# A memset between the scattered and gathered transfers, in place of waits, in an audio tower with a mixture of experts

## The chip, the cores and the metric

The kernel runs on one core of a Trainium2 chip. The metric is the device time of one execution in microseconds. It has five engines with a queue each: PE (matmul), DVE (vector), ACT (scalar), POOL (GpSimd) and SP, which here only issues DMAs. Transfers with a list of rows (indirect DMAs) are issued by POOL, the others by SP and ACT.

## The reference, cut to what matters

Tokens are 128 sequences of 63 positions with 64 channels. A depthwise convolution with a norm and an activation comes first, then a state-space block, then a mixture of 64 experts, of which each token uses two.

```python
def _L0_ffn_ref(x, Wr, br, W1, b1, W2, b2):
    logits = xf @ Wr + br
    topk_logits, topk_idx = jax.lax.top_k(logits, TOP_K)          # TOP_K = 2
    gates = jax.nn.softmax(topk_logits, axis=1)
    combine = jnp.zeros((T, E), xf.dtype).at[jnp.arange(T)[:, None], topk_idx].add(gates)
    for e in range(E):                                            # E = 64
        h = jax.nn.relu(xf @ W1[e] + b1[e])
        y = h @ W2[e] + b2[e]
        out = out + combine[:, e:e + 1] * y
...
h = _L0_tok_ref(x, ...)
h = h + _L0_attn_ref(_layernorm(h, axis=-1), ...)
h = h + _L0_ffn_ref(_layernorm(h, axis=-1), ...)
```

## The kernel before

Partitions are sequences, the free axis is positions and channels. The convolution and the state-space block (POOL, DVE, ACT and PE together) take the first half of the time. The change is in what follows.

**Routing.** The 63 positions are cut into eight groups of 8 (the last has 7) and into three shares, SHARES = (0, 16), (16, 40), (40, 63): groups 0 and 1, groups 2 to 4, groups 5 to 7. For each group ACT normalises, PE makes the logits, DVE picks the two best experts (`choose`, which counts s_hot up) and PE counts tokens for each expert. For each share DVE then computes where each token's row goes in a list sorted by expert (`slots_of`, `rows_of`: L1547 writes slot_i and counts s_slot up) and which expert each tile of that list belongs to.

**Scatter.** `send` (L625) has POOL write the rows of a share into its `sorted_rows` in DRAM: one indirect DMA for each position and choice, 128 rows of 256 bytes each, so 2 x 63 = 126 in all (32, 48 and 46 for the three shares). A share's rows may be read once its s_disp is full.

**Expert steps.** 80 steps, 24, 28 and 28 for the shares; a step takes two pairs of tiles of 128 rows. PE transposes the rows (`rows_T`, L887), multiplies with W1 (`hidden`, L897) two loops later and with W2 (`outputs`, L906) four loops later, so there are 84 loops. ACT copies (L1162) and applies half of the relu (L1167), DVE does the other half (L1595) and copies the outputs (`y_copy`, L1604), which counts s_dstep up. ACT issues the loads of sorted rows, a unit of two steps at a time and some steps ahead (`next_rows`): the first unit of the second share in loop 17, that of the third in loop 45, and there it waits for that share's s_disp. It also issues the store of each step's outputs to `expert_out`. SP loads the weights of each tile, 96.5 KB, 11 steps ahead at most.

**Gather.** For each share, POOL waits until all of its steps are stored (s_st), and then gathers the rows of `expert_out` back with one indirect DMA for each position and choice (L651), 126 again. Behind the steps PE and ACT make the bias part (s_cb), DVE adds it (L1653, s_cbc) and then adds the gathered rows times their gates (L1645, L1647), group by group of OUTS; SP stores.

**The pace.** POOL's order is scatter of shares 0, 1, 2, then gather of shares 0, 1, 2. Transfers are numbered d = 0 to 251 in this order. `keep_pace(d)` (L616) stands ahead of each: at six of the scatters it waits until a group has been chosen (GROUP_AT: transfer 18 for the third group, ..., 44 for the eighth), from d = 62 on at every second one it waits until the steps have come to (d - 60) x 80 / 153 (STEP_AT), and from 212 on at every third for a bias add (BIAS_AT). `Chain.link` (L137) makes an instruction count a semaphore up and makes the engine wait for the new count ahead of its next instruction.

Of the kernel before, what the change touches and what calls it, by code (L numbers as in the profile page):

```python
# [15 lines left out]
P = 128  # L16
# [3 lines left out]
L = 63  # L20
# [23 lines left out]
SHARES = ((0, 16), (16, 40), (40, L))  # L44
# [23 lines left out]
PAIR0, UNIT0, STEP0 = ([sum(v[:h]) for h in range(len(SHARES) + 1)] for v in (PAIRS, UNITS, STEPS))  # L68
# [4 lines left out]
IDS = 32  # L73


FIRST_STEP = 44
LAG = 16
EVERY = 2
GROUP_AT = {18: 3, 21: 4, 25: 5, 38: 6, 41: 7, 44: 8}
STEP_AT = {d: (d - FIRST_STEP - LAG) * STEP0[-1] // 153 for d in range(FIRST_STEP + LAG + EVERY, FIRST_STEP + LAG + 154, EVERY)}  # L80
BIAS_AT = {212 + 3 * q: q + 1 for q in range(CQ)}


# [39 lines left out]
def dve_rounds(steps):  # L123
    return steps + LATE - LAG_H
# [18 lines left out]
def build(nc, x, w, b, gamma, beta, alpha, A_log, D_param, scale, W_dt, b_dt, W_B, b_B, W_C, b_C,  # L143
# [5 lines left out]
    with ExitStack() as ctx:  # L149
        def sb(name, shape, dt=F32):  # L150
            return ctx.enter_context(nc.sbuf_tensor(name, shape, dt))

        def sem(name):
            return ctx.enter_context(nc.semaphore(name))
# [47 lines left out]
        tile_e = sb("tile_e", [P, len(SHARES)])  # L202
        te = sb("te", [1, len(SHARES) * P], I32)
        b2w = sb("b2w", [P, P])

        uT = xt[0:C + 1, 0:3 * GL * P].rearrange("p (k n) -> p k n", k=3)
        dt = dt_t[:, :]
# [115 lines left out]
        s_hot = sem("s_hot")  # L323
# [15 lines left out]
        s_dstep = sem("s_dstep")  # L339
# [119 lines left out]
        def _(pool):  # L459
            ch = Chain(pool, s_pool)  # L460
# [154 lines left out]

            def keep_pace(d):  # L616

                if d in GROUP_AT:
                    pool.wait_ge(s_hot, GROUP_AT[d])
                if d in STEP_AT:  # L620
                    pool.wait_ge(s_dstep, dve_rounds(STEP_AT[d]))
                if d in BIAS_AT:
                    pool.wait_ge(s_cbc, BIAS_AT[d])

            def send(h, g):  # L625

                for c in range(2):
                    for l in range(span_of(g).start, span_of(g).stop):
                        keep_pace(2 * span_of(g).start + c * (span_of(g).stop - span_of(g).start) + l - span_of(g).start)
                        pool.indirect_dma_start(  # L630
                            out=sorted_rows[h], out_offset=bass.IndirectOffsetOnAxis(ap=slot_i[:, c, l:l + 1], axis=0),
                            in_=xn[:, l, :], in_offset=None).then_inc(s_disp[h], 16)
# [9 lines left out]
            for h in range(len(SHARES)):  # L642
                for j in range(YRING):
                    pool.wait_ge(s_st[j], 16 * ((STEP0[h + 1] + YRING - 1 - j) // YRING))
                for g, (a, z) in enumerate(OUTS):
                    if not SHARES[h][0] <= a < SHARES[h][1]:
                        continue
                    for c, y in enumerate((y1, y2)):
                        for l in range(a, z):
                            keep_pace(2 * L + 2 * a + c * (z - a) + l - a)  # L650
                            pool.indirect_dma_start(  # L651
                                out=y[:, l, :], out_offset=None, in_=expert_out[h],
                                in_offset=bass.IndirectOffsetOnAxis(ap=slot_i[:, c, l:l + 1], axis=0)
                            ).then_inc(s_yl[c][g], 16)
# [1028 lines left out]
```

## Time and profile before

| | |
|---|---|
| median of 3 runs | 863.99 us (858.28 to 868.59) |
| the profiled execution | 861.92 us, span from the first to the last instruction 859.9 us |
| busy | PE 60%, DVE 65%, ACT 38%, POOL 70% of the span |
| mean granted TensorE clock | 0.767 of full speed |

A row of a timeline gives the start and the duration in us, the engine, the line of the kernel, the operation, what it writes and reads with partitions x elements, how many instructions are merged in the row, and in brackets how long the engine had been idle before it and which instruction's signal ended that idle time. "remote" and "issue" there mean that the profile shows no instruction that the engine waited for. An indirect DMA's row on POOL is POOL's part of it (it prepares the transfer), not the movement of the data. A row of stretches gives, for each engine, busy us with the count of instructions that begin in the stretch, then the granted TensorE clock, the busy share of the DMA engines and the GB/s that they moved.

### The profile page before, as it was taken

What the parts mean: (1) busy time and instruction counts of PE and PEld (TensorE: products, weight loads), DVE (VectorE), ACT (ScalarE), POOL (GpSimd) and SP (SyncE); (2) the same over time, 40 slices, a digit from 0 to 9 for tenths busy, and PEclk for the clock granted to TensorE, in tenths of its full rate; (3) what the DMA queues carried; (4) which work ended last, traced back from release to release, by engine and by line L of the source; (5) the groups of instructions that cost most, each with busy time, mean ns of one, the idle gap of its engine ahead of it and who ended that gap; (6) DMA issues with size and microseconds to landing.
All of it is one profiled execution on the core that took longest, in us unless ns stands there. A gap on an engine that the chain in (4) does not pass through costs nothing.

```text
span 859.9 us, 8932 instructions
## 1 busy us (share of the span) xinstructions
PE 512.3 (60%) x2514; PEld 334.2 (39%) x2520; DVE 561.7 (65%) x1180; ACT 323.0 (38%) x622; POOL 599.8 (70%) x393
## 2 busy tenths in 40 slices
PE   4744237576556666775736766777777783787100
PEld 4743112122222222223413435655666573676100
DVE  1597899999999999997726662444444452333072
ACT  2159856556556655534211312222222331322000
POOL 5995789999999999980464464655555545563764
PEclk9958567878788779676756876888888996879555
DMA  7999990000000000000135023867877985741121
GB/s 235 382 180 123 78 4 0 1 0 0 0 0 0 0 0 0 0 0 1 41 83 138 15 72 91 228 197 217 237 223 207 251 256 144 211 127 50 26 81 51
DMA packets 106604, 84.95 MB, mean 99 GB/s; under 512 B 30464, under 2 KB 90240, under 8 KB 106560
## 3 DMA queue, kind: packets, MB, share of 16 engines
q1 hardware_dynamic: 79312, 54.76, 30.5%
q10 hardware_dynamic: 19184, 21.40, 8.3%
q0 software_dynamic: 8064, 8.27, 3.9%
q8 instruction: 19, 0.31, 0.2%
q14 instruction: 25, 0.20, 0.1%
HBM read 57.22 MB, written 33.49 MB: 105 GB/s over the span
## 4 chain that ended last, share of the span: by engine, by line
PE 29%; POOL 21%; DVE 18%; issue 12%; another core or an unknown queue 10%; ACT 7%; SPq 1%; POOLq 0%; DMA 0%; ACTq 0%; DVEq 0%
POOL w_ring L571 9%; POOL x_w L578 9%; PE ps L906 9%; PE ps L897 6%; PE ps L887 5%; DVE hh_ring L1419 4%; DVE x_w L1595 2%; PE ps L740 2%; POOL xt L651 2%; PE ps L676 2%; ACT ps L1072 2%; DVE x_w L1604 1%; DVE mi L1507 1%; DVE lstat L1290 1%
## 5 line engine op out<-in xcount | busy, mean ns | idle before, releaser
L740 PE MATMUL ps<-x_w,ident 128*128 128x512 f32 x252 | 162.1, 804 | 92.5 <-POOL x_w L578 92.5
L630 POOL DMA_INDIRECT sorted_rows<-xp,slot_i x126 | 123.5, 980 | 117.5 <-DVE x_w L1604 35.4
L651 POOL DMA_INDIRECT xt<-expert_out,slot_i x126 | 123.0, 976 | 89.7 <-issue 33.2
L571 POOL TENSOR_TENSOR w_ring<-xt,bc 128x2016 f32<-128x2016 f32 x32 | 143.0, 4471 | 13.4 <-DVE hh_ring L1419 7.3
L1419 DVE TENSOR_TENSOR_SCAN hh_ring<-ps,w_ring 128x1024 f32<-128x1024 f32 x64 | 145.9, 2279 | 0.1
L578 POOL TENSOR_TENSOR x_w<-hh_ring,bc 128x2016 f32<-128x2016 f32 (+1 forms) x32 | 140.7, 4399 | 1.1 <-PE ps L740 1.1
L740 PEld LDWEIGHTS ps<-x_w,ident 128*128 128x128 f32 x252 | 62.7, 259 | 194.5 <-POOL x_w L578 116.9
L1162 ACT ACTIVATE x_w<-ps 128x256 f32<-128x256 f32 x80 | 30.9, 386 | 205.2 <-PE ps L887 93.6
L1072 ACT ACTIVATE ps<-dt_t,a_exp 128x1024 f32<-128x1024 f32 x64 | 71.5, 1117 | 64.2 <-DVE hh_ring L1419 64.2
L1066 ACT ACTIVATE ps<-dt_t,a_exp 128x1024 f32<-128x1024 f32 x64 | 71.5, 1118 | 52.1 <-DVE w_ring L1398 52.0
L1398 DVE TENSOR_TENSOR w_ring<-ps,w_ring 128x1008 f32<-128x1008 f32 x64 | 76.8, 1200 | 3.4 <-ACT ps L1066 3.4
L1413 DVE SCALAR_TENSOR_TENSOR w_ring<-ps,w_ring 128x1008 f32<-128x1008 f32 x64 | 75.6, 1182 | 0.0
L1595 DVE TENSOR_SCALAR x_w<-ps,dt_t 128x128 f32<-128x128 f32 x70 | 21.5, 346 | 67.4 <-PE ps L887 36.0
L906 PE MATMUL ps<-dt_t,x_w 128*128 128x128 f32 x280 | 46.9, 319 | 29.7 <-DVE x_w L1604 29.2
L1595 DVE TENSOR_SCALAR x_w<-ps,x_w 128x128 f32<-128x128 f32 x56 | 17.3, 346 | 66.7 <-remote 37.0
L906 PE MATMUL ps<-x_w 128*128 128x128 f32 x224 | 37.9, 321 | 33.0 <-DVE x_w L1604 23.9
L906 PEld LDWEIGHTS ps<-dt_t,x_w 128*128 128x128 f32 x280 | 42.5, 231 | 32.3 <-ACT x_w L1167 31.5
L906 PEld LDWEIGHTS ps<-x_w 128*128 128x128 f32 x224 | 34.4, 233 | 35.5 <-ACT x_w L1167 33.8
L887 PE MATMUL ps<-ident,x_w 128*128 128x128 f32 x160 | 40.8, 343 | 1.5 <-issue 1.5
L1604 DVE COPY x_w<-ps 128x256 f32<-128x256 f32 x80 | 33.2, 415 | 0.9 <-PE ps L906 0.7
L740 PE MATMUL ps<-hh_ring,ident 128*128 128x512 f32 x16 | 11.1, 832 | 33.2 <-ACT hh_ring L1055 26.0
L897 PE MATMUL ps<-x_w,dt_t 64*128 64x128 f32 x280 | 30.2, 339 | 0.0
(209 smaller groups left out, 904.1 us busy)
## 6 DMA issues: line engine op xcount, KB each, us to landing
dt_t<-packed SPq DMA_DIRECT2D x140, 96.5 KB
x_w<-packed SPq DMA_DIRECT2D x112, 96.5 KB
x_w<-sorted_rows ACTq DMA_DIRECT2D x40, 256.0 KB
expert_out<-x_w ACTq DMA_DIRECT2D x80, 128.0 KB
sorted_rows<-pad_rows SPq DMA_DIRECT2D x2, 3584.0 KB, 24.1
bc<-packed SPq DMA_DIRECT2D x68, 96.5 KB
packed<-in_L_ffn_W SPq DMA_DIRECT2D x3, 2048.0 KB, 42.0
x_w<-in_x SPq DMA_DIRECT2D x7, 448.0 KB, 9.5
```

Source lines behind the costliest of these rows:

```text
L571: pool.tensor_tensor(w_buf(k, 2), up3[:, bass.ds(c * DC, DC), 1:S].unsqueeze(1).broadcast_to([P, 2, DC, L]), vec_of(k, 2), ALU.mult).then_ ...
L578: pool.tensor_tensor(hc_buf(k, n), h_buf(k, n), vec_of(N + k, n), ALU.mult).then_inc(s_hcp, n)
L630: pool.indirect_dma_start(out=sorted_rows[h], out_offset=bass.IndirectOffsetOnAxis(ap=slot_i[:, c, l:l + 1], axis=0), in_=xn[:, l, :], in_ ...
L651: pool.indirect_dma_start(out=y[:, l, :], out_offset=None, in_=expert_out[h], in_offset=bass.IndirectOffsetOnAxis(ap=slot_i[:, c, l:l + 1] ...
L740: ins = pe.matmul(ps[:, i, :], ident[:, :], src[:, i * BANK:(i + 1) * BANK], start=(k < 0), stop=(k == (N - 2 if last else N - 1)), skip_g ...
L887: last = pe.transpose(ps[:, i % 2, j * P:(j + 1) * P], rows_in[:, u % RING, in_share(n) % UNIT, :], ident[:, :])
L897: last = pe.matmul(ps[:, 2 + 2 * (i % 2) + t, j * P:(j + 1) * P], w_of(n)[t * C:(t + 1) * C, t, 0:HID], xT_e[t * C:(t + 1) * C, i % 2, j, ...
L906: last = pe.matmul(ps[:, 6 + i % 2, (2 * j + t) * OUT:(2 * j + t + 1) * OUT], hT_e[:, i % 2, t, j, :], w_of(n)[:, t, HID + C - OUT:HID + C ...
L1072: act.activation(banks(2 + 2 * (k % 2), 2), d, ACT.Exp, scale=a_exp[:, 1, k:k + 1]).then_inc(s_dA, 1)
L1398: dve.tensor_tensor(wv, body(banks(6, 2)), wv, ALU.mult).then_inc(s_g, 1)
L1413: dve.scalar_tensor_tensor(out=wv, in0=body(dA), scalar=1.0, in1=wv, op0=ALU.add, op1=ALU.mult).then_inc(s_b, 1)
L1419: dve.tensor_tensor_scan(hh_ring[:, k % 4, :], dA, w_ring[:, k % 4, :], 0.0, ALU.mult, ALU.add).then_inc(s_h, 1)
```

## The change

The waits for chosen groups and for steps go. In their place POOL writes zeros into a scratch of 128 x 128, `beat`, ahead of every transfer below number 2 x (63 + 40) = 206, that is, all scatters and the gathers of the first two shares, and waits for that write's own count before the transfer. The waits for bias adds (from number 212 on) stay.

```diff
-FIRST_STEP = 44
-LAG = 16
-EVERY = 2
-GROUP_AT = {18: 3, 21: 4, 25: 5, 38: 6, 41: 7, 44: 8}
-STEP_AT = {d: (d - FIRST_STEP - LAG) * STEP0[-1] // 153 for d in range(FIRST_STEP + LAG + EVERY, FIRST_STEP + LAG + 154, EVERY)}
 BIAS_AT = {212 + 3 * q: q + 1 for q in range(CQ)}
...
         b2w = sb("b2w", [P, P])
+        beat = sb("beat", [P, P])
...
             def keep_pace(d):
 
-                if d in GROUP_AT:
-                    pool.wait_ge(s_hot, GROUP_AT[d])
-                if d in STEP_AT:
-                    pool.wait_ge(s_dstep, dve_rounds(STEP_AT[d]))
+                if d < 2 * (L + SHARES[-1][0]):
+                    ch.link(pool.memset(beat[:, :], 0.0))
                 if d in BIAS_AT:
                     pool.wait_ge(s_cbc, BIAS_AT[d])
```

## Rows read from the trace of the kernel before

**Rows 1.** The page: span, busy us, the chain by engine, POOL's transfers (mean ns).

```profile
span 859.9 us, 8932 instructions
PE 512.3 (60%) x2514; PEld 334.2 (39%) x2520; DVE 561.7 (65%) x1180; ACT 323.0 (38%) x622; POOL 599.8 (70%) x393
...
PE 29%; POOL 21%; DVE 18%; issue 12%; another core or an unknown queue 10%; ACT 7%; SPq 1%; POOLq 0%; DMA 0%; ACTq 0%; DVEq 0%
...
L630 POOL DMA_INDIRECT sorted_rows<-xp,slot_i x126 | 123.5, 980 | 117.5 <-DVE x_w L1604 35.4
L651 POOL DMA_INDIRECT xt<-expert_out,slot_i x126 | 123.0, 976 | 89.7 <-issue 33.2
```

**Rows 2.** Stretches by stage, all engines (busy us, count; clock, DMA share, GB/s).

```profile
418.00:478.50 60.50, 32.13 (x168) 19.44 (x169) 30.43 (x140) 14.48 (x39) 31.20 (x32) 0.63 0.35 93
478.50:514.00 35.50, 22.74 (x141) 14.51 (x143) 22.53 (x98) 9.06 (x23) 22.31 (x23) 0.76 0.16 51
514.00:782.50 268.50, 194.19 (x1440) 164.20 (x1440) 108.31 (x380) 70.57 (x240) 147.45 (x151) 0.82 0.70 194
782.50:859.90 77.40, 12.81 (x96) 11.64 (x96) 27.47 (x44) 4.67 (x8) 45.54 (x46) 0.60 0.18 49
```

**Rows 3.** Stretches of the steps, L1604 alone: one copy for each step.

```profile
558.50:640.50 82.00, 10.37 (x25) 0.85 0.77 216
...
692.50:700.70 8.20, 1.66 (x4) 1.00 0.92 268
```

**Rows 4.** Timelines of three bursts: POOL's first (and last), what resumed behind it.

```profile
541.73 1.01 POOL L630 DMA_INDIRECT sorted_rows<-xp,slot_i  x1 [2.16 <-DVE x_w L1604]
...
548.16 0.97 POOL L630 DMA_INDIRECT sorted_rows<-xp,slot_i  x1 [0.30 <-issue]
...
550.45 0.38 ACT L1162 ACTIVATE x_w<-ps 128x256 f32<-128x256 f32 x1 [4.23 <-PE ps L887]
...
700.72 0.95 POOL L651 DMA_INDIRECT xt<-expert_out,slot_i  x1 [8.18 <-DMA expert_out<-x_w]
...
717.08 0.95 POOL L651 DMA_INDIRECT xt<-expert_out,slot_i  x1 [0.30 <-issue]
...
720.80 0.38 ACT L1162 ACTIVATE x_w<-ps 128x256 f32<-128x256 f32 x1 [14.87 <-remote]
...
786.35 0.95 POOL L651 DMA_INDIRECT xt<-expert_out,slot_i  x1 [10.79 <-DMA expert_out<-x_w]
...
820.54 1.46 DVE L1653 TENSOR_TENSOR hg<-ps,hg 128x512 f32<-128x512 f32 x2 [16.93 <-remote]
```

**Rows 5.** Timeline of routing: the first scatter; ACT's counts copy, behind it.

```profile
417.96 1.17 POOL L630 DMA_INDIRECT sorted_rows<-xp,slot_i  x1 [21.16 <-DVE slot_i L1547]
...
447.99 0.28 ACT L1123 ACTIVATE counts<-ps 128x128 bf16<-128x128 f32 x1 [15.20 <-remote]
```

**Rows 6.** Timeline of POOL at the kernel's start: two linked memsets.

```profile
2.97 0.20 POOL L470 MEMSET ones<- 128x128 f32 x1
3.24 0.20 POOL L471 MEMSET tri<- 128x128 f32 x1
```

**Rows 7.** Timeline: slots of the second share and the transfer waiting; third share's slots.

```profile
478.08 0.21 DVE L1547 TENSOR_TENSOR slot_i<-w_ring 128x48 int32<-128x48 int32 x1
...
478.57 0.97 POOL L630 DMA_INDIRECT sorted_rows<-xp,slot_i  x1 [10.95 <-DVE slot_i L1547]
...
512.72 0.25 DVE L1547 TENSOR_TENSOR slot_i<-w_ring 128x46 int32<-128x46 int32 x1
```

**Rows 8.** One stretch of pairs of transfers: first L1604 alone, then POOL alone.

```profile
751.70:762.00 10.30, 1.78 (x5) 0.83 0.69 196
...
751.70:762.00 10.30, 6.67 (x7) 0.83 0.69 196
```

**Rows 9.** Timeline of POOL in the tail: its wait for a bias add; last transfer.

```profile
821.56 0.95 POOL L651 DMA_INDIRECT xt<-expert_out,slot_i  x1 [5.31 <-DVEq L1654]
...
849.65 0.95 POOL L651 DMA_INDIRECT xt<-expert_out,slot_i  x1 [0.30 <-issue]
```

## The prediction

> **What bounds the kernel now.** Read the page first: POOL is the busiest engine (70% of the span), yet the chain that ended last names PE, POOL, DVE and much "issue" and "unknown" beside each other [rows 1]: no engine is full, so the answer is in a stage. The table by stages shows where POOL's transfers lie: 32 while the first two groups' rows are scattered and routing goes on, 23 while routing ends, 151 during the 80 expert steps, 46 behind them [rows 2]. That is all 126 scatters and 126 gathers. The steps take 268.5 us, 3.36 us each, with PE at 194 of 268 us; the tail behind them takes 77 us. The other stages are routing, and the work before 418 us, which the change doesn't touch.
>
> Now look for what ends the idle time in the steps. Between 692.5 and 700.7 us POOL waits for stores and issues nothing: there four step ends fall into 8.2 us, 2.05 each, at a granted clock of 1.00. Between 558.5 and 640.5 us, with POOL issuing in bursts of six, it is 25 in 82 us, 3.28 each, at 0.85 [rows 3]. So the work is not the bound, and neither is the weight traffic, which ran at 268 GB/s in the good stretch. What is lost goes to hand-offs between engines. Compare three bursts: 6 transfers begin at 541.73 and ACT gets its next matmul result at 550.45; 14 begin at 700.72 and ACT, idle for 14.87 us, resumes at 720.80; 24 begin at 786.35 and DVE, idle for 16.93, resumes at 820.54 [rows 4]. That is 8.72/6 = 1.45, 20.08/14 = 1.43 and 34.19/24 = 1.42 us for a transfer, although POOL issues one every 1.26 (in the burst of 14: 16.36 us for 13 spacings). Something behind POOL digests a transfer in 1.42 us; back-to-back issue builds a backlog of about 0.15 us per transfer, and after a few of them the other engines' signals wait until the backlog is empty. Routing has the same block: ACT's counts copy at 447.99 us stood idle 15.20 us behind the first burst [rows 5].
>
> The waits that the change removes are what keeps the bursts short: inside the steps POOL issues six, and waits for DVE's step counter until the others have caught up.
>
> **The change, part by part.** Removed: six waits for s_hot (transfers 18 to 44) and 76 for s_dstep (transfers 62 to 212, every second one). They were satisfied by other engines' progress, so their cost was POOL standing still; nothing else is queued behind them on POOL but the next transfers. Unchanged: s_slot, s_st and BIAS_AT.
>
> Added: a 128x128 memset ahead of each transfer with d below 2 x (63 + 40) = 206: all 126 scatters and the 80 gathers of the first two shares. Through `link` it adds to s_pool and the next instruction, the transfer, waits for that. So POOL can't issue a transfer before the memset has run and signalled, and the memset stands in order behind the transfer before. The scratch `beat` is read by nobody; no DMA is added, and no other queue waits on s_pool any more (SP's only wait on it is 5, at the start).
>
> The price of one transfer, t, from start to start. The transfer itself is 0.97 us in most rows [rows 7], 0.98 in the mean [rows 1]. A memset of this shape is 0.205 us, and two linked ones start 0.27 us apart, so a linked instruction costs a gap of about 0.07 [rows 6]. A transfer that waits for another instruction starts 0.28 us after that one ends (478.29 to 478.57) [rows 7]. Unknown is the gap from a transfer to a memset: no row of before has that pair. Bounds: 0.07 as between memsets, and 0.30 as between transfers. So t lies between 0.97 + 0.07 + 0.205 + 0.28 = 1.525 and 1.755; I take a gap of 0.175, t = 1.63, in the middle, because the 0.30 before a transfer must hold both the end of the last one and the start of the next, of which the memset meets only the first. Every value is over the 1.42 us of the digestion, so no backlog is built. The nearest row for what steps do at such a spacing: between 751.7 and 762 us two transfers and a pause alternate, seven in 10.3 us (1.47 each), and five steps end in the same time [rows 8]; with the fence posts counted against me 10.3/4 = 2.6 us a step, where six in a row had given 3.28.
>
> With that POOL is the bound from its first scatter at 418 us on [rows 5]. By transfers: share 0's 32 scatters end at 418 + 32 x 1.63 = 470; share 1's 48 at 548; share 2's 46 at 623; the 32 gathers of share 0 at 675, the 48 of share 1 at 754. Is POOL ever held up? Share 1's slots are there at 478.29 in before [rows 7], 8 us after 470; but the 15.20 us block in that stage [rows 5] goes, so I take no wait (8 us is the bound). Share 2's slots came at 513 [rows 7]. ACT's loads of share 1's rows wait for its scatters in step 17, at 514 + 17 x 2.6 = 558, past 548; of share 2's in step 45, 631, past 623. Share 0's stores are done by loop 28, 587; share 1's by loop 56, 660; the 84 loops by 514 + 84 x 2.6 = 732, all ahead of POOL. The steps would have to take (754 - 514)/84 = 2.86 us each to hold the end.
>
> The last share's 46 gathers have no memset. In before they took from 786.35 to the span's end, 73.5 us [rows 2, 4], of which 5.3 us is POOL's wait for a bias add that its own burst had held up [rows 9]. In after the biases are done before the burst starts, so that wait goes; but all 46 stand in one burst, whose backlog (46 x 0.16 = 7 us) is drained at the end, where before it was a burst of 22, from 821.56 to 849.65 (3.5) [rows 9]. I take 72.
>
> Sum: 418 + 206 x 1.63 + 72 = 826, and 2.0 around the span (861.92 for a span of 859.9): 828 against 861.92. The median of the runs is 2.1 above the profiled execution, so the forecast is 830. At the bounds of t: 806 and 854. Break-even: (862 - 74 - 418)/206 = 1.80 us.
>
> **The rivals.** *The memset starts only when the transfer is digested* (slower). The 1.42 us may be POOL's own time for a transfer, with the profile's 0.97 only its visible part: then the memset runs behind it, t = 1.42 + 0.205 + 0.28 = 1.905, and the end is 418 + 206 x 1.905 + 74 = 884 (886 beside the median), 2.6% slower. It decides from t = 1.80 on. For it: the drains fit 1.42 per transfer with nothing left over [rows 4]. Against it: 13 transfers in a row were issued every 1.26 us with no back-pressure, and the others' first hand-offs in a burst pass at once. The Trainium skill speaks for this one: Perfetto Trace Analysis, DMA Instruction — SWDGE (GPSIMD), says that the reported end of such a DMA is the last descriptor's write and that the DSP finishes its binary after that, and the section on GPSIMD instructions says not to trust spans there but the spacing of starts; by that rule t is 1.9 and the end 884. The spacing of starts in this trace is 1.26, not 1.42, so the trace doesn't bear it out; 0.19.
>
> *The steps don't get faster* (the time stays). With POOL busy all the time a hand-off may still be late at every transfer, where bursts at least left pauses. At 3.2 us for each of 84 loops the steps end at 514 + 268 = 782 as before, POOL waits for the last stores, and the time is 862 whatever t is. For it: the stretch of 1.47 spacing is only 10 us long, and holds pauses. Against it: no backlog. 0.13.
>
> *The memset is held up by more than one transfer*, because s_pool's signal is as late as the others' are in a burst: t of 2 and more, over 900. Only one transfer is outstanding, so it has little for it: 0.06.
>
> **The numbers.** The forecast holds 0.62; its own range is 802 to 857 (t's bounds and 4 us of the tail). About 1% is what a measurement of this kernel can tell from no change; faster by over 1% is t under 1.755. Faster: 0.61 of the forecast and 0.02 of steps only half improved, 0.63. The same: 0.01 + 0.11 + 0.02 = 0.14. Slower: 0.19 + 0.04 = 0.23. The range over all: 802 to 892; about 0.04 lies below and 0.1 above.
>
> **What would show it.** Starts of transfers below d = 206 spaced 1.53 to 1.76 us with a 0.2 us memset between (1.9 would be the rival); no idle of ACT or DVE over 3 us ended by PE in the steps; step ends 2 to 2.6 us apart; share 0's gathers starting near 623 and the last share's near 754, with no wait for stores ahead of them; POOL at over 75% busy behind 418 us. I am wrong if POOL waits for stores again ahead of the last share (the steps are the bound), or if the spacing is over 1.8.

## The result, and the profile after

The changed kernel takes 881.75 us (median; 880.9 to 885.0), the kernel before, measured beside it, 863.8: a ratio of 1.022 (95% interval 1.018 to 1.026). The change is a loss of 18 us, where the forecast was a gain of 34. The profiled execution of the changed kernel is 885.0 us, the slowest of its four, its span 883.3.

The page of the changed kernel comes first, as [rows 1] of the kernel before: span, busy time of each engine, the chain by engine, and POOL's three groups (count, busy us, mean ns, idle time ahead of them and what ended most of it).

```profile
span 883.3 us, 9136 instructions
...
PE 527.1 (60%) x2514; PEld 339.6 (38%) x2520; DVE 562.4 (64%) x1180; ACT 324.2 (37%) x622; POOL 645.1 (73%) x599
...
PE 27%; POOL 25%; DVE 14%; issue 14%; another core or an unknown queue 13%; ACT 4%; DMA 1%; POOLq 0%; SPq 0%; DVEq 0%; ACTq 0%
...
L645 POOL DMA_INDIRECT xt<-expert_out,slot_i x126 | 123.1, 977 | 68.2 <-issue 33.4
...
L624 POOL DMA_INDIRECT sorted_rows<-xp,slot_i x126 | 123.5, 980 | 35.9 <-POOL beat L615 19.5
...
L615 POOL MEMSET beat<- 128x128 f32 x206 | 45.2, 219 | 82.3 <-DMA expert_out<-x_w 50.6
```

POOL is busier (73%), yet it stands still for long: 82.3 us ahead of memsets, of which 50.6 are ended by stores of the steps' outputs, and 68.2 ahead of gathers. Before, most of its idle time in the steps was ended by DVE's step counter (35.4 us ahead of scatters [rows 1]); now it is ended by stores that the steps have not yet made.

The stretches, as [rows 2] (us, then busy us and count for PE, PEld, DVE, ACT, POOL, then granted clock, DMA share, GB/s):

```profile
418.00:478.50 60.50, 37.88 (x182) 22.07 (x183) 33.90 (x163) 16.33 (x44) 40.70 (x68) 0.67 0.35 94
478.50:514.00 35.50, 22.70 (x139) 14.07 (x142) 20.38 (x77) 6.85 (x16) 28.77 (x49) 0.74 0.15 52
514.00:782.50 268.50, 184.59 (x1265) 151.33 (x1263) 97.83 (x343) 62.68 (x209) 174.91 (x295) 0.74 0.67 184
782.50:883.30 100.80, 33.18 (x270) 29.55 (x270) 38.60 (x79) 14.03 (x39) 46.93 (x47) 0.66 0.22 63
```

The stretch from 514 to 782.5 held the 80 steps before, with PE busy for 194 us at a clock of 0.82. Now it holds 1265 of PE's matmuls in place of 1440, at a clock of 0.74, while POOL begins 295 instructions there, memsets among them, in place of 151. Behind it lie 270 matmuls in place of 96 [rows 2], so some 175 of the steps' matmuls now come later. It is the steps that became slower. The copy that ends a step (L1598, L1604 before) shows how much, as in [rows 3]: first a stretch in which POOL scatters without a pause, then one in which it waits for stores.

```profile
524.00:612.00 88.00, 7.46 (x18) 0.66 0.56 153
686.00:713.00 27.00, 5.81 (x14) 1.00 0.97 281
```

18 steps in 88 us are 4.9 us each; 14 in 27 us are 1.93 each, with the clock at 1.00. The kernel before, with its bursts of six, took 3.28 [rows 3].

The timeline shows why, and what it leads to (start, duration, engine, line, what; in brackets the idle time and what ended it):

```profile
475.08 0.25 POOL L615 MEMSET beat<- 128x128 f32 x1 [10.37 <-DVE slot_i L1541]
...
543.30 0.44 PE L881 MATMUL ps<-ident,x_w 128*128 128x128 f32 x2
543.51 0.98 POOL L624 DMA_INDIRECT sorted_rows<-xp,slot_i  x1 [0.28 <-issue]
544.49 0.22 POOL L615 MEMSET beat<- 128x128 f32 x1
544.98 0.98 POOL L624 DMA_INDIRECT sorted_rows<-xp,slot_i  x1 [0.28 <-issue]
545.96 0.22 POOL L615 MEMSET beat<- 128x128 f32 x1
546.00 0.38 ACT L1156 ACTIVATE x_w<-ps 128x256 f32<-128x256 f32 x1 [5.00 <-remote]
546.00 0.61 DVE L1589 TENSOR_SCALAR x_w<-ps,dt_t 128x128 f32<-128x128 f32 x2 [4.46 <-remote]
546.52 0.41 DVE L1598 COPY x_w<-ps 128x256 f32<-128x256 f32 x1
547.08 2.04 PE L900 MATMUL ps<-dt_t,x_w 128*128 128x128 f32 x8 [3.35 <-DVE x_w L1598]
...
629.66 0.20 POOL L615 MEMSET beat<- 128x128 f32 x1 [15.14 <-DMA expert_out<-x_w]
...
712.65 0.21 POOL L615 MEMSET beat<- 128x128 f32 x1 [35.46 <-DMA expert_out<-x_w]
...
809.00 0.95 POOL L645 DMA_INDIRECT xt<-expert_out,slot_i  x1 [25.76 <-DMA expert_out<-x_w]
```

Three things are to be read from it. The memset's row starts at the very end of the transfer's row ahead of it (543.51 + 0.98 = 544.49; 544.98 + 0.98 = 545.96), and the transfers are 1.47 us apart. The profile's rows on POOL are rough at their edges; the spacing of the starts is the safe figure. PE's transposes end at about 543.74 (the ends of PE's rows are modelled), but ACT and DVE, which wait for the count that PE gives behind them, both begin at 546.00, 2.3 us later: at this spacing the hand-off is held, as in the bursts of [rows 4]. It is the hand-off from PE that is late. The one back to PE is not: DVE's copy ends at 546.93, and PE begins at 547.08, 0.15 us later, as it does in most steps of this stretch. The prediction speaks of the other engines' signals; every one that is held in the rows shown here and in [rows 4, 5] waits for PE. And POOL, ahead of the steps all the time, waits 10.4 us for the slots of the second share and then 15.1, 35.5 and 25.8 us for the stores of the three shares, 86.7 in all. The last share's gathers start at 809.00, where before they started at 786.35 [rows 4].

That ACT and DVE begin in the same instant also tells what this is not. The Trainium skill, SBUF — State Buffer, section SBUF: two separate sides, says that POOL and DVE share a pair of ports of which one locks the other out, and that ACT has none of it. ACT is held like DVE here, so that lock is not what these rows show.

### The profile page after: what moved, and what is told of

It reads as the page before. It is cut to its first block, busy times and chain, and to the rows that moved or that the text cites. A ratio compares the mean times of both kernels' runs of the same rounds, so it can differ in the third digit from the quotient of the medians.

```text
span 883.3 us, 9136 instructions
## 1 busy us (share of the span) xinstructions
PE 527.1 (60%) x2514; PEld 339.6 (38%) x2520; DVE 562.4 (64%) x1180; ACT 324.2 (37%) x622; POOL 645.1 (73%) x599
## 4 chain that ended last, share of the span: by engine, by line
PE 27%; POOL 25%; DVE 14%; issue 14%; another core or an unknown queue 13%; ACT 4%; DMA 1%; POOLq 0%; SPq 0%; DVEq 0%; ACTq 0%
POOL x_w L574 14%; POOL w_ring L567 10%; PE ps L900 8%; PE ps L891 5%; PE ps L881 4%; POOL xt L645 2%; PE ps L670 2%; DVE x_w L1589 2%; PE ps L734 1%; DVE mi L1501 1%; PE ps L761 1%; PE ps L756 1%; DVE x_w L1598 1%; DVE lstat L1284 1%
## 5 line engine op out<-in xcount | busy, mean ns | idle before, releaser
L734 PE MATMUL ps<-x_w,ident 128*128 128x512 f32 x252 | 159.2, 793 | 94.9 <-POOL x_w L574 94.9
L645 POOL DMA_INDIRECT xt<-expert_out,slot_i x126 | 123.1, 977 | 68.2 <-issue 33.4
L615 POOL MEMSET beat<- 128x128 f32 x206 | 45.2, 219 | 82.3 <-DMA expert_out<-x_w 50.6
L900 PE MATMUL ps<-dt_t,x_w 128*128 128x128 f32 x280 | 49.6, 331 | 32.1 <-DVE x_w L1598 20.1
L900 PEld LDWEIGHTS ps<-dt_t,x_w 128*128 128x128 f32 x280 | 44.3, 240 | 36.4 <-ACT x_w L1161 22.9
L1589 DVE TENSOR_SCALAR x_w<-ps,bc 128x128 f32<-128x128 f32 x34 | 10.6, 346 | 40.5 <-PE ps L881 20.3
L900 PE MATMUL ps<-bc,x_w 128*128 128x128 f32 x136 | 24.4, 331 | 19.1 <-issue 11.5
```

Of the source, the lines that this page charges most:

```text
L645: pool.indirect_dma_start(out=y[:, l, :], out_offset=None, in_=expert_out[h], in_offset=bass.IndirectOffsetOnAxis(ap=slot_i[:, c, l:l + 1] ...
L734: ins = pe.matmul(ps[:, i, :], ident[:, :], src[:, i * BANK:(i + 1) * BANK], start=(k < 0), stop=(k == (N - 2 if last else N - 1)), skip_g ...
L900: last = pe.matmul(ps[:, 6 + i % 2, (2 * j + t) * OUT:(2 * j + t + 1) * OUT], hT_e[:, i % 2, t, j, :], w_of(n)[:, t, HID + C - OUT:HID + C ...
```

## The experiments

Two readings stood against each other at first. By "room", signals pass only in what the spacing of the transfers leaves over the 1.42 us of the digestion; the changed kernel leaves 1.474 - 1.42 = 0.05 us. By "grid", a signal passes at every third or fourth transfer, whatever their spacing (the release at 546.00, 0.04 us behind a transfer's end, speaks for it; of ACT's fifteen other waits that end between 524 and 612 six end so, the others elsewhere). A third, "write", blames the memset itself. All ratios are against the kernel before, measured on the same chip. The runs come from four chips, on which the kernel before took 858.1 to 863.8 us, so times of different runs are compared to within 1% at best.

**A longer memset.** The one size that sets the spacing:

```diff
-        beat = sb("beat", [P, P])
+        beat = sb("beat", [P, 256])
```

> The changed kernel with a scratch of 128x256 in place of 128x128. By the columns a memset grows by 0.11 us (from 0.219; estimate from 0.205 for 128x128 and 0.525 for 128x512 in the trace of before), so the spacing of transfers goes from 1.474 to about 1.58 us. Theory 'room': a transfer is digested in 1.42 us and the other engines' signals pass only in what the spacing leaves over; the room goes from 0.05 to 0.16 us a transfer, so the steps that took 5.9 us between 524 and 612 take 4 or less, the waits for stores ahead of the gathers (76 us in all) fall under 30, and the time is 835 to 865. Rival 'grid': a signal passes at every third or fourth transfer, whatever their spacing; then a step is 4 x 1.58 = 6.3 us and the time is about 900. Rival 'write': the memset itself holds the others up (it writes SBUF beside DVE); a longer one is worse, over 890.

Measured: 816.3 us, a ratio of 0.955 (0.945 to 0.964). The three views, POOL's timeline, the steps' copies in a stretch where the rows are there, and the longest wait of the stretch from 524 to 612 (line waited for: us, times, longest):

```profile
541.45 0.98 POOL L624 DMA_INDIRECT sorted_rows<-xp,slot_i  x1 [0.28 <-POOL beat L615]
542.43 0.33 POOL L615 MEMSET beat<- 128x256 f32 x1
543.03 0.98 POOL L624 DMA_INDIRECT sorted_rows<-xp,slot_i  x1 [0.28 <-POOL beat L615]
```

```profile
640.00:700.00 60.00, 11.83 (x29) 1.00 0.89 261
```

```profile
ACT x_w L1156 <- DMA sorted_rows<-xp,slot_i: 24.4, 1, 24.4
```

It is faster than any of the three readings had it. (The expectations take 5.9 us for a step of the changed kernel between 524 and 612; the 18 copies above give 4.9.) 0.11 us more for each transfer, and the steps end 60/29 = 2.07 us apart at full clock while POOL issues without a pause. They are now so fast that they wait for the next share's rows, 24.4 us at once. Grid and write fall: both asked for a slower kernel. No wait of POOL for stores or slots is left behind 418 us.

**A still longer one**, 128x512:

> The changed kernel with a scratch of 128x512: a memset of about 0.54 us, a spacing of about 1.79 us. Room: 0.37 us a transfer are left over; steps of 3 us or less where both stages run, POOL is then the bound from its first scatter at 418 us on and never waits for stores for long: 418 + 206 x 1.79 + 74 = 861, range 855 to 875. Grid: 4 x 1.79 = 7.2 us a step, 920 to 940. Write: worse than with 128x256 and over 900.

Measured: 860.4 us, a ratio of 1.006 (1.003 to 1.010).

```profile
540.72 0.97 POOL L624 DMA_INDIRECT sorted_rows<-xp,slot_i  x1 [0.28 <-POOL beat L615]
541.69 0.54 POOL L615 MEMSET beat<- 128x512 f32 x1
542.50 0.97 POOL L624 DMA_INDIRECT sorted_rows<-xp,slot_i  x1 [0.28 <-POOL beat L615]
```

The spacing is 1.79 us, and POOL is the bound all the way. The prediction's break-even was a spacing of 1.80; this run lies on it.

**None at all**, the wait taken away without anything in its place:

```diff
             def keep_pace(d):
 
-                if d < 2 * (L + SHARES[-1][0]):
-                    ch.link(pool.memset(beat[:, :], 0.0))
                 if d in BIAS_AT:
```

> The changed kernel without the memset: neither waits for groups and steps nor a write ahead of a transfer (the waits for bias adds stay), so transfers follow one another every 1.27 us. Room: less than nothing is left over, each back-to-back stretch builds a backlog, and steps stand nearly still in it; slower than the changed kernel's 882, 890 to 950. Grid: a step is 4 x 1.27 = 5.1 us in place of 5.9, so faster than 882, about 862. Write: without the memset the steps are faster, under 870.

Measured: 964.7 us, a ratio of 1.129 (1.117 to 1.142), a little slower than the range that was expected. Its bursts are as long as the shares, and give the digestion once more. First and last scatter of the first share, and what ACT does next:

```profile
417.92 1.17 POOL L622 DMA_INDIRECT sorted_rows<-xp,slot_i  x1 [21.45 <-DVE slot_i L1539]
...
457.53 0.96 POOL L622 DMA_INDIRECT sorted_rows<-xp,slot_i  x1 [0.30 <-issue]
...
462.90 0.28 ACT L1115 ACTIVATE counts<-ps 128x128 bf16<-128x128 f32 x1 [30.15 <-remote]
```

32 transfers are issued in 40.6 us, and ACT, idle for 30.15 us, resumes 44.98 us after the first one began: 1.41 us for each, as in [rows 4]. The movement of the data is not what takes 1.41 us. In this trace the packets of POOL's DMA queue, 32 for a transfer, follow one another at 1.27 us a transfer, as they are issued, and the share's last one ends at 459.64, 3.3 us before ACT resumes.

**Between 1.474 and 1.58**: the sizes 128x192 and 128x160.

> The changed kernel with a scratch of 128x192. Between the two runs with 128x128 (memset 0.219, spacing 1.474, 882 us) and 128x256 (0.327, 1.58, 816 us) this gives a memset of 0.273 and a spacing of 1.53 us at the scatters, 1.50 at the gathers: the lower bound of the spacing in the prediction. Room: 1.53 is still over the 1.42 of the digestion by twice what 1.474 was; the steps run at 1.9 to 2.6 us, POOL is the bound and 206 x 0.053 = 11 us are saved against 128x256: 805, range 800 to 815. If the steps need more room than 0.1 us a transfer, they are late again and the time is 820 to 860.

Measured: 804.9 us, a ratio of 0.935 (0.929 to 0.941). This is the fastest of all the kernels here.

```profile
540.56 0.27 POOL L615 MEMSET beat<- 128x192 f32 x1
541.11 0.97 POOL L624 DMA_INDIRECT sorted_rows<-xp,slot_i  x1 [0.28 <-POOL beat L615]
542.08 0.27 POOL L615 MEMSET beat<- 128x192 f32 x1
542.63 0.98 POOL L624 DMA_INDIRECT sorted_rows<-xp,slot_i  x1 [0.28 <-POOL beat L615]
```

```profile
524.00:612.00 88.00, 14.04 (x34) 0.92 0.89 256
```

> The changed kernel with a scratch of 128x160: a memset of 0.246, a spacing of 1.50 us at the scatters, 1.48 at the gathers. If the digestion is 1.42 and any room is enough, POOL is the bound: 816 - 206 x 0.08 = 800. If what matters is how much is left over, it stands between 128x128 and 128x192, with steps of 3 to 5 us and waits for stores ahead of the gathers: 815 to 860.

Measured: 819.2 us, a ratio of 0.951 (0.945 to 0.957).

```profile
524.00:612.00 88.00, 12.02 (x29) 0.88 0.86 240
```

The edge has a width. In the same 88 us there are 18 steps at a spacing of 1.474 us, 29 at 1.50 and 34 at 1.53 (of which one waited 10.7 us for rows). With 128x160 POOL still waits for stores, 13.0 and 9.7 us; with 128x192 no more.

**The columns without the bytes**: a scratch of one partition.

```diff
-        beat = sb("beat", [P, P])
+        beat = sb("beat", [1, 256])
```

> The changed kernel with a scratch of 1 partition x 256 in place of 128x128: the columns, and so by the rows the memset's time, are those of 128x256, and 1/128 of its bytes are written. Room: only the spacing matters, 816 (810 to 823). Write (the bytes that POOL writes beside DVE have a price or a use): another time than 816, by more than 1%.

Measured: 811.9 us, a ratio of 0.943 (0.937 to 0.949). It is not the 816 of 128x256, but the memset was not as long either, 0.304 in place of 0.327 us, so the transfers are 1.55 apart, and 206 x 0.023 = 4.7 us is the difference. With 1/128 of the bytes written the time is what the spacing gives; an effect of the bytes is not seen.

**The wait for the count moved** from the transfer to the next memset:

```diff
-                    ch.link(pool.memset(beat[:, :], 0.0))
+                    pool.wait_ge(ch.sem, ch.at)
+                    pool.memset(beat[:, :], 0.0).then_inc(ch.sem, 1)
+                    ch.at = ch.at + 1
```

(with a scratch of 128x256).

> A memset of 128x256 ahead of each transfer, but the wait for its count stands ahead of the next memset, not of the transfer, so the transfer follows the memset without a wait for it. If the 0.28 us between a memset's end and the transfer's start are the transfer's own start (0.30 stood between two transfers that waited for nothing): spacing 1.58 as with the wait, 816 (810 to 823). If they are the price of the wait: spacing 1.35 to 1.45, under the digestion, steps late, over 880.

Measured: 898.9 us, a ratio of 1.047 (1.043 to 1.050).

```profile
540.20 0.33 POOL L616 MEMSET beat<- 128x256 f32 x1
540.70 0.98 POOL L626 DMA_INDIRECT sorted_rows<-xp,slot_i  x1 [0.16 <-issue]
541.67 0.34 POOL L616 MEMSET beat<- 128x256 f32 x1
542.17 0.97 POOL L626 DMA_INDIRECT sorted_rows<-xp,slot_i  x1 [0.17 <-issue]
```

```profile
524.00:612.00 88.00, 5.80 (x14) 0.67 0.45 123
```

The transfer starts 0.17 us behind the memset in place of 0.28: 0.17 is its own start, 0.11 the price of the wait. The spacing falls to 1.465 us, a little more than expected and just below the changed kernel's, and so does the pace: 14 steps in 88 us. The memset is half as long again as the changed kernel's, yet the result lies beside it, and not beside the other run with 128x256: the length of the memset is not the cause, and the spacing is what the two slow runs share.

**Only one stage lengthened**: 128x256 ahead of scatters, 128x128 ahead of gathers.

```diff
-                    ch.link(pool.memset(beat[:, :], 0.0))
+                    ch.link(pool.memset(beat[:, 0:256 if d < 2 * L else P], 0.0))
```

> A memset of 128x256 ahead of the 126 scatters, and of 128x128, as in the changed kernel, ahead of the 80 gathers, whose spacing was 1.45 us there (their digestion 1.42 to 1.43 by the bursts of before). Room, with the same limit for gathers: the steps run up to the end of the scatters, about 622 us, and are late during the gathers of the first two shares, at 5 to 7 us each, so POOL waits for stores ahead of the second share's or the last share's gathers; 835 to 875. If gathers at 1.45 leave room enough (the loss of the changed kernel was all in the scatters): 816 - 80 x 0.107 = 808.

Measured: 837.8 us, a ratio of 0.973 (0.969 to 0.977).

```profile
765.73 0.95 POOL L645 DMA_INDIRECT xt<-expert_out,slot_i  x1 [29.82 <-DMA expert_out<-x_w]
```

```profile
622.00:668.00 46.00, 4.15 (x10) 0.69 0.64 170
```

The scatters run as in the run with 128x256; then 80 gathers, most of them 1.45 us apart, hold up the steps (10 in 46 us), and POOL waits 29.8 us for the last stores. So gathers have a limit too, near that of the scatters; whether it is the same one is not shown.

**One half of the change**, routing alone: the memset of 128x128 up to transfer 61, the waits for steps kept.

```diff
-                if d in GROUP_AT:
-                    pool.wait_ge(s_hot, GROUP_AT[d])
+                if d < FIRST_STEP + LAG + EVERY:
+                    ch.link(pool.memset(beat[:, :], 0.0))
                 if d in STEP_AT:
```

> One half of the change alone: the waits for chosen groups go and the memset of 128x128 stands ahead of transfers 0 to 61; the waits for steps stay as in the kernel before, with no memset behind 61. The changed kernel had the slots of the second share about 3 us earlier than the kernel before. Room: the loss of the changed kernel is in the steps, so this half is no loss: 0.985 to 1.0 of the kernel before. Rival (the loss starts in routing): over 1.01.

Measured: 841.1 us, a ratio of 0.979 (0.972 to 0.986). The write of the second share's slots, which came at 478.08 before [rows 7], and the steps:

```profile
468.14 0.21 DVE L1548 TENSOR_TENSOR slot_i<-w_ring 128x48 int32<-128x48 int32 x1
```

```profile
514.00:763.00 249.00, 182.50 (x1407) 154.39 (x1407) 104.58 (x364) 68.75 (x232) 140.38 (x144) 0.86 0.73 207
```

This half is a gain by itself, more than was expected (0.985 to 1.0): slots 10 us earlier, the first step's copy at 513.9 in place of 531.0, and the last share's gathers at 763.39 in place of 786.35 [rows 4]. So the other half, the steps, costs some 41 us against it.

**Both paces**, all the old waits and the memset as well:

```diff
                 if d in STEP_AT:
                     pool.wait_ge(s_dstep, dve_rounds(STEP_AT[d]))
+                if d < 2 * (L + SHARES[-1][0]):
+                    ch.link(pool.memset(beat[:, :], 0.0))
```

> The kernel before with all its waits, and the memset of 128x128 added ahead of each transfer below number 206, so that the bursts between the waits are spaced 1.47 us in place of 1.27. Room: what lets the steps run are the pauses, and the spacing in a burst hardly matters; a burst of six takes 1.2 us longer, but leaves as much less to digest behind it; within 1.5% of the kernel before (851 to 877). Grid: about the same. Write: 206 memsets cost the steps time, 875 or more.

Measured: 829.9 us, a ratio of 0.971 (0.961 to 0.981); no theory had expected that.

The first step's copy and the first of the last share's gathers:

```profile
508.95 0.41 DVE L1607 COPY x_w<-ps 128x256 f32<-128x256 f32 x1
...
754.62 0.95 POOL L654 DMA_INDIRECT xt<-expert_out,slot_i  x1 [8.59 <-DMA expert_out<-x_w]
```

In the kernel before the two stand at 531.01 and 786.35. So the last gathers come 31.7 us earlier; 22.1 of these are the earlier first step, which the routing stage gives, and only 9.6 are faster steps (245.7 us from the one row to the other in place of 255.3). An account of the faster steps that no run tests: at a spacing of 1.27 a hand-off waits for the end of the burst; at 1.47 some pass inside it, and the old waits still give a pause when the steps fall behind. Without those pauses the same spacing is the changed kernel's loss.

All the runs with one memset size up to transfer 205 and no waits for groups or steps, against the prediction's own sum, 418 + 126 x t(scatter) + 80 x t(gather) + 74, with the measured spacings:

| scratch | spacing, scatter and gather (us) | steps' copies from 524 to 612 | sum (us) | measured (us) |
|---|---|---|---|---|
| 128x256, wait behind | 1.465, 1.445 | 14 | 792 | 898.9 |
| 128x128 (the change) | 1.474, 1.45 | 18 | 794 | 881.75 |
| 128x160 | 1.50, 1.475 | 29 | 799 | 819.2 |
| 128x192 | 1.53, 1.505 | 34 | 805 | 804.9 |
| 1x256 | 1.55, 1.53 | 29, rows awaited | 810 | 811.9 |
| 128x256 | 1.58, 1.56 | 29, rows awaited | 816 | 816.3 |
| 128x512 | 1.79, 1.77 | 27, rows awaited | 859 | 860.4 |

From 1.53 us on the sum holds within 2 us; below, the steps are the bound. (The run with only the scatters lengthened has a sum of 807 and took 837.8: the 30 us between are its wait for the last stores.) An estimate from the four upper rows says how much room a step needs: at 4.9 us a step there are 4.9/1.474 = 3.3 transfers in it, which leave 3.3 x 0.054 = 0.18 us over the 1.42. In the same way the first row gives 6.3 us, 4.3 transfers and 0.19 us, the third 3.0, 2.0 and 0.16, the fourth (without the 10.7 us of waiting) 2.3, 1.5 and 0.16. By this estimate a step takes some 0.16 to 0.19 us of what the transfers leave over, and is as slow as it takes to collect it. The figure hangs on the third digit of the digestion (with 1.41 it is 0.18 to 0.24, with 1.43 it is 0.14 to 0.15), and part of a slow step is the lower clock (see the last section), so the order of the runs is shown, and the law is not.

## Why the prediction was wrong, point by point

**The reading of before was right.** Back-to-back transfers are digested more slowly than they are issued and hold up the other engines: the run without any pace shows it at its worst, and 32 transfers in it give 1.41 us each. That the work itself is not the bound is shown by 1.93 us a step where POOL is silent. What is held up is narrower than the prediction had it, the hand-offs from PE.

**Two steps failed. The first is the price of the spacing.** The prediction took 1.63, between 1.525 and 1.755, and put 0.07 to 0.30 us between the end of a transfer and the memset behind it. The trace of the changed kernel has 0.00 there. The other terms were as told: 0.98 for the transfer (0.97 told), 0.22 for the memset (0.205 told), 0.28 to the next transfer. So t is 1.474, below the lower bound. The prediction said that no row of before had that pair, and still bounded the gap below by 0.07; bounded by nothing, t would have been 1.455 at least. This step alone is not the loss: in the prediction's own sum 1.474 gives 794, a larger gain.

**The second, which turned the gain into a loss, is a limit without a width.** "Every value is over the 1.42 us of the digestion, so no backlog is built" was used as a yes or no, and steps of 2.6 us were taken to follow. At 1.474 the spacing is also over, by 0.05, and the steps took 4.9 us: what the transfers leave over must be enough for the steps' hand-offs. The row behind the 2.6 us misled: the 1.47 us of [rows 8] is a mean over pairs of transfers and pauses, and at an even 1.474, without pauses, the steps were nearly twice as slow. With the prediction's lower bound of t the conclusion would have held: at 1.53 us the steps took 2.6 us, the number it had from [rows 8] (with a wait for rows in them, so that they agree is partly luck), and the time, 804.9, is that of its lower bound, 806.

**The sum** was right wherever POOL is the bound, and so was its break-even (1.80; at 1.79 the time is 860.4). With 128x192 the agreement is partly luck, as two terms were off against each other: the last share's gathers start at 737.5, where the spacings alone give 731, since a few transfers take 1.4 us and more, and the tail from there takes 68.5 in place of 72. The bias wait goes in that run, as told; in the changed kernel it is there again, 5.4 us, since the steps end too late. For the changed kernel the sum with the true spacing is 794, and the four waits of POOL that it told away, 86.7 us, make 880. They are those of the profiled execution, which took 885.0; the rest is a transfer mean of 1.478 us in place of the common spacings and a tail of 74.3 us in place of 72.

**The rivals.** The first, a memset that starts only when the transfer is digested (t = 1.905, 886), came nearest in time and is wrong in its mechanism: the transfers are 1.474 us apart, which leaves no place for a memset behind 1.42 us. The rule of the Trainium skill beside it (Perfetto Trace Analysis, DMA Instruction — SWDGE (GPSIMD)), that the instruction runs on behind its reported end, adds nothing that can be seen here: 0.00 us between the two rows. The third falls with it. The second, steps that don't get faster, was the right kind, hand-offs late at every transfer and POOL waiting for the last stores, and was priced as no worse than before (3.2 us a step, 862). It is worse, because the old bursts came with pauses in which steps ran at full pace, and an even spacing just over the digestion has none. What it named as its cause, a POOL that is always busy, is not it: with 128x192 POOL is busy all the time too.

**Routing** did what was told (no wait for slots was expected) only in the runs with more room: with 128x192 the second share's slots come at 458.70, in the changed kernel at 474.81, where POOL waited 10.4 us.

**What stays open**: what it is behind POOL that digests a transfer and holds the signals; no view here names it, and the data has moved by then. Nor is it shown whether PE's signal is late or its last matmul, since the ends of PE's rows are modelled. And why the changed kernel had the second share's slots at 474.81, while the run of the routing half, the same instructions up to there, had them at 468.14; so near the limit, small shifts may do it, but no run shows that.

## What to carry to other kernels

In this kernel, where indirect transfers were issued faster than they were digested, PE's hand-offs to ACT and DVE were late. Where a trace shows the like, measure the digestion from a long burst (first start to the first hand-off behind it), and space the transfers over it with some margin, here 1.53 us for 1.41 to 1.42, as the other work must fit into what is left. Here a spacing just over the limit was worse than bursts with pauses, one 4% longer was the best of all, and beyond that each 0.01 us cost 2 us, so sweep it. And when a forecast has a cliff in it, ask on which side of the cliff the bounds of each term put it, the bound of nothing too.

## What had not been expected of the hardware

By the profile's rows a memset on POOL begins in the instant at which the transfer ahead of it ends (0.00 us), while a transfer behind a memset takes 0.17 us to start, and 0.28 if it waits for the memset's count. A memset of 1x256 takes 0.304 us, one of 128x256 0.327. And the edge is steep: from 1.474 to 1.50 us between transfers, 2% of the spacing, the time falls by 7%.

The clock has a part in the slow steps. All engines of the changed kernel, first with transfers 1.474 us apart, then with POOL silent:

```profile
524.00:612.00 88.00, 56.30 (x322) 44.78 (x322) 26.29 (x92) 16.04 (x54) 70.75 (x119) 0.66 0.56 153
686.00:713.00 27.00, 27.00 (x257) 23.61 (x256) 20.11 (x72) 12.81 (x43) 0.21 (x1) 1.00 0.97 281
```

In the first stretch the granted clock is 0.66, a mean of the two levels of 1.2 and 2.4 GHz; PE, idle for 2 to 3 us in most steps there, then needs 2.05 us for the eight matmuls of the second layer that take 1.06 at the full clock. An estimate from these rows: PE is busy for 56.30/18 = 3.1 us a step in place of 27.00/14 = 1.9, and idle for 1.8 in place of none. So of the 3 us that a step loses some 1.2 are slower matmuls and 1.8 are idle time; the clock's part comes with the idle time, and no run separates the two. With 128x256, from 640 to 700, PE is not held, and the clock is 1.00.
